# A linear-attention layer on eight cores: four of five weight loads split into staged pieces on other queues

## The reference

```python
# x: (8, 4096, 1024) f32; all weights (1024, 1024) f32
def attn(x):                                  # causal linear attention, 16 heads of 64
    q, k, v = x @ Wq.T, x @ Wk.T, x @ Wv.T
    q, k = phi(rope(q)), phi(rope(k))         # phi(x) = elu(x) + 1
    # per token t: K_sum += k_t; KV += k_t (x) v_t; y_t = (q_t KV) / max(q_t . K_sum, 1e-6)
    return Y @ Wo.T
x = x + attn(layernorm(x))
x = x + layernorm(x) @ sign(Wf).T
```

## Time and profile before

| | us |
|---|---|
| median of the runs | 1230.93 |
| the profiled execution | 1231.27 |
| its span on the slowest core (core 2) | 1229.7 |
| spans of the 8 cores | 1224.3 to 1229.7 |
| busy in the span: TensorE / VectorE / ScalarE / GpSimd | 905.9 / 689.6 / 492.1 / 160.4 |

### The profile page before, as it was taken

The page is one execution under the profiler, slowest core; times in us unless marked ns, Lnnn a source line. Parts: engine busy times, 40 slices in busy tenths (PEclk is TensorE's granted clock), DMA queues, the critical chain, the costliest instruction groups (busy, mean ns, idle before and its releaser), DMA issues.

```text
span 1229.7 us, 33733 instructions; the slowest of 8 cores (1224.3 to 1229.7 us)
## 1 busy us (share of the span) xinstructions
PE 905.9 (74%) x13571; PEld 829.4 (67%) x13571; DVE 689.6 (56%) x1514; ACT 492.1 (40%) x991; POOL 160.4 (13%) x139
## 2 busy tenths in 40 slices
PE   1428787877878787787878778787777787877775
PEld 1417776766777676677767667777667776866775
DVE  5225555566555556655555665554566555556653
ACT  2134433444443344444334444433444434344341
POOL 1201110011111001111100111110011111001110
PEclk9859989899998989999898999988989989898996
DMA  9871011011000101010110111010011001001000
GB/s 167 129 117 36 19 37 36 19 36 36 33 22 36 36 18 36 36 36 19 36 36 19 36 36 36 19 36 28 26 36 37 28 27 36 25 30 36 19 13 24
DMA packets 15144, 46.77 MB, mean 38 GB/s; under 512 B 1424, under 2 KB 1424, under 8 KB 14992
## 3 DMA queue, kind: packets, MB, share of 16 engines
q1 hardware_dynamic: 9504, 33.62, 7.7%
q0 software_dynamic: 5488, 11.01, 5.9%
HBM read 38.86 MB, written 16.78 MB: 45 GB/s over the span
## 4 chain that ended last, share of the span: by engine, by line
DVE 29%; PE 27%; issue 23%; ACT 11%; DMA 6%; POOL 1%; DVEq 1%; ACTq 0%; POOLq 0%
PE att L496 6%; PE pjA L496 6%; PE pjB L496 6%; PE pjC L496 6%; DVE junkV L404 4%; DVE Asb L629 4%; DVE x L712 4%; DVE outb L728 3%; DMA wk<-wkT 3%; ACT kev L510 3%; ACT qT L475 2%; PE ptr L448 2%; DMA wf<-wfT 2%; DVE ln L441 2%; ACT YT L700 2%
## 5 line engine op out<-in xcount | busy, mean ns | idle before, releaser
L526 POOL TENSOR_TENSOR rA<-qev,tabS_s 128x512 bf16<-128x512 bf16 x32 | 37.0, 1157 | 882.9 <-ACT qev L510 813.0
L496 PE MATMUL att<-wo,YT 128*128 128x128 bf16 x544 | 98.8, 258 | 7.7 <-ACT YT L700 7.7
L496 PE MATMUL pjC<-wo,YT 128*128 128x128 bf16 x480 | 86.3, 255 | 23.2 <-ACT YT L700 23.2
L496 PE MATMUL pjA<-wo,YT 128*128 128x128 bf16 x544 | 98.3, 257 | 6.6 <-ACT YT L700 6.6
L496 PE MATMUL pjB<-wo,YT 128*128 128x128 bf16 x480 | 86.2, 254 | 5.7 <-ACT YT L700 5.7
L496 PE MATMUL att<-wv,ln1T 128*128 128x128 bf16 x512 | 68.1, 224 | 19.9 <-ACT kev L510 13.1
L496 PE MATMUL att<-wq,ln1T 128*128 128x128 bf16 x512 | 77.1, 228 | 6.2 <-DMA wq<-wqT 6.2
L496 PE MATMUL pjC<-wv,ln1T 128*128 128x128 bf16 x512 | 67.6, 220 | 17.9 <-ACT kev L510 17.9
L496 PE MATMUL pjB<-wf,ln2T 128*128 128x128 bf16 x512 | 77.8, 224 | 0.8 <-ACT ln2T L454 0.8
L496 PE MATMUL pjB<-wv,ln1T 128*128 128x128 bf16 x512 | 66.7, 219 | 15.4 <-ACT kev L510 15.4
L496 PE MATMUL pjA<-wv,ln1T 128*128 128x128 bf16 x512 | 66.5, 221 | 15.1 <-ACT kev L510 15.1
(11 more groups left out here) (152 smaller groups left out, 3043.6 us busy)
## 6 DMA issues: line engine op xcount, KB each, us to landing
xs<-x SPq DMA_DIRECT2D x32, 512.0 KB, 3.7
out<-outb SPq DMA_DIRECT2D x32, 512.0 KB, 2.6
wq<-wqT POOLq DMA_DIRECT2D x1, 2048.0 KB, 22.3
wk<-wkT POOLq DMA_DIRECT2D x1, 2048.0 KB, 34.1
wv<-wvT POOLq DMA_DIRECT2D x1, 2048.0 KB, 47.1
wo<-woT POOLq DMA_DIRECT2D x1, 2048.0 KB, 18.4
wf<-wfT POOLq DMA_DIRECT2D x1, 2048.0 KB, 25.8
tabS_s<-tabS POOLq DMA_DIRECT2D x1, 256.0 KB, 27.4
```

Source lines behind the costliest of these rows:

```text
L496: s.add("tensor", lambda e, o=o, i=i, pj=pj, off=off, lsb=lsb, w_sb=w_sb: e.matmul(pj[:, off:off + 128], lsb[:, i * 128:(i + 1) * 128], w_ ...
L526: s.add("gpsimd", lambda e: e.tensor_tensor(out=rAv, in0=HI, in1=Sb, op=ALU.mult), reads=[src_res, "tabS"], writes=["rA"], tag=f"{tag}_rA")
```

## The change

The load of wq stays one casting DMA on GpSimd. wk, wv, wo and wf are each cut in 8 pieces, one for each block of 128 input rows. A piece is a plain f32 DMA of 0.52 MB into a staging buffer, followed by a cast into the bf16 weight. wk and wv go through SyncE's queue into the two f32 buffers `x2` and are cast by VectorE; wo and wf go through ScalarE's queue into the two f32 buffers `outb` and are cast by ScalarE itself. Piece p therefore waits until piece p-2 on the same queue is cast. Each block of a weight becomes a resource of its own, and a matmul waits for its block `i` only. The sign over wf stays one instruction and reads all 8 blocks. The declared costs are 1400 for a piece's DMA, 800 for a cast on VectorE and 1400 on ScalarE.

```diff
-        for wsb, wdram, name, weng in ((wq, wq_d, "wq", "gpsimd"),
-                                       (wk, wk_d, "wk", "gpsimd"),
-                                       (wv, wv_d, "wv", "gpsimd"),
-                                       (wo, wo_d, "wo", "gpsimd"),
-                                       (wf, wf_d, "wf", "gpsimd")):
-            s.add(weng,
-                  lambda e, a=wsb, b=wdram: e.dma_start(
-                      out=a[:].rearrange("p (a o) -> p a o", a=8),
-                      in_=b.rearrange("(a p) o -> p a o", p=128)),
-                  writes=[name], dma=True, tag=f"load_{name}", cost=7000)
+        s.add("gpsimd",
+              lambda e: e.dma_start(
+                  out=wq[:].rearrange("p (a o) -> p a o", a=8),
+                  in_=wq_d.rearrange("(a p) o -> p a o", p=128)),
+              writes=[f"wqb{i}" for i in range(8)], dma=True,
+              tag="load_wq", cost=7000)
+        for wsb, wdram, name, qeng, ceng, stg in (
+                (wk, wk_d, "wk", "sync", "vector", x2),
+                (wv, wv_d, "wv", "sync", "vector", x2),
+                (wo, wo_d, "wo", "scalar", "scalar", outb),
+                (wf, wf_d, "wf", "scalar", "scalar", outb)):
+            for i in range(8):
+                sb = stg[i % 2]
+                sres = f"stg_{id(stg) % 97}_{i % 2}"
+                s.add(qeng,
+                      lambda e, sb=sb, b=wdram, i=i: e.dma_start(
+                          out=sb[:],
+                          in_=b.rearrange("(a p) o -> p a o", p=128)[:, i, :]),
+                      writes=[sres], dma=True, tag=f"load_{name}p{i}", cost=1400)
+                if ceng == "vector":
+                    fn = (lambda e, sb=sb, a=wsb, i=i:
+                          e.tensor_copy(a[:, i * D:(i + 1) * D], sb[:]))
+                else:
+                    fn = (lambda e, sb=sb, a=wsb, i=i:
+                          e.copy(a[:, i * D:(i + 1) * D], sb[:]))
+                s.add(ceng, fn, reads=[sres], writes=[f"{name}b{i}"],
+                      tag=f"cast_{name}p{i}", cost=800 if ceng == "vector" else 1400)
         s.add("scalar", lambda e: e.sign(wf[:], wf[:]),
-              reads=["wf"], writes=["wf"], tag="sign_wf")
+              reads=[f"wfb{i}" for i in range(8)],
+              writes=[f"wfb{i}" for i in range(8)], tag="sign_wf")
 ...
+            wresi = [f"{wres}b{i}" for i in range(8)]
 ...
-                        reads=[lresA if i < 4 else lresB, wres],
+                        reads=[lresA if i < 4 else lresB, wresi[i]],
```

## The result

The changed kernel takes 1241.15 us in the median of 11 runs, against 1231.3 before (10 runs). The ratio is 1.0075, 95% interval 1.006 to 1.0091: some 9 us slower, 7 to 11 by the interval. The forecast was 1228, a gain. The profiled execution took 1240.08 us, with a span of 1238.4 on core 0, against 1231.27 and 1229.7.

The account below looks back on a forecast made before the run. The prediction took a loading stage of about 92 us and 31 unchanged periods as the bound. From 1231.27 it took 6.2 us for an earlier YT and added 3.0 for exposed sign and casts: 1228.1, range 1214 to 1246.

Parts of the forecast that it names:

- What bounds the kernel: Whole kernel: a loading stage of about 92 us, then 31 chunk periods of 35.88 us on average, unchanged.
- Who gets the bandwidth: Loading stage: queues share 336 GB/s; wq lands at 24 to 30 us, wv's last piece at 71.
- The work of the DMA engines: Loading stage: 23.6 MB at 336 GB/s takes 70 us; last piece lands at 73 against 84.5 before.
- The path from wv to YT: Chunk 0: cast, v projection, evacuations and 7.7 us more put YT at 85.5 against 91.67, 6.2 us earlier.
- The sign and the casts: ScalarE behind YT: two casts and the sign, 9.2 us, meet a 6.33 us gap; 3 us exposed.
- ScalarE's list becomes the bound: Rival, loading stage: wo and wf pieces waited for singly, sign ahead of v's evacuation, YT at 103; 1235 to 1247, chance 0.13.
- Nothing is gained: Rival, loading stage: three lists leave as much loose DMA time; wv lands at 77, time 1230 to 1234, chance 0.17.
- The order of the periods: Rival, chunk periods: the schedule may settle in another order, 0.8 us per period, 25 us in all; chance 0.05.

Follow-up runs that it names:

- one-queue kernel: Kernel before, sign behind LN1 of chunk 1 and in eight pieces, all GpSimd loads issued ahead of rotations, seven DMA semaphores for three: 1214.92 us.
- held-back wo: Changed kernel with the first two pieces of wo issued only behind the last cast of wk: 1244.55 us.
- third buffer: Changed kernel with three staging buffers in place of two for wk and wv, x's loads for chunks 1 and 2 moving too: 1233.65 us.
- place of x: Changed kernel with two buffers, the loads of x for chunks 1 and 2 issued behind the pieces of wv: 1237.02 us.
- real costs: Changed kernel with planner costs near measured lengths, 3300 for a SyncE piece (was 1400), 30000 for wq (was 7000): 1242.94 us.

## Why the prediction was wrong

**What bounds the kernel.** Right: a loading stage and periods that don't change. The residual of chunk 1 carries the whole difference. In the profiled executions the forecast of 1228.1 missed 1240.1 by 12.0 us: 8.8 in YT of chunk 0, 4.6 in the sign and the casts behind it, less 1.4 in the rest.

**Who gets the bandwidth.** The step that failed. That queues share the engines was right, the sizes were not. The sum let wq land at 24 to 30 us and then gave SyncE's queue half of 336 GB/s: 14 pieces from 29 us at 3.1 us each. It began as forecast: by 28 us SyncE's queue had moved 2.58 MB of its 9.96. But all three queues together moved 305 GB/s there and not 336 (casting writes counted twice, as f32 read): 99 by SyncE's and 80 by ScalarE's, where 79 were taken for each, so 125 were left for the casting queue. wq landed at 37.2 (1.6 + 35.6) and the second table at 45.6, and from 29 us until then three queues shared where the sum had two. From 28 to 79.7 us SyncE's queue moved 144 GB/s in place of 168, so its pieces took 3.7 us each. wk's last cast was expected near 46 and came at 50.3, wv's at 70 to 73 and came at 79.7. With ScalarE's queue held back until wk was cast, the three moments were 28.3, 43.0 and 70.0, as forecast or earlier, and in the changed kernel the last cast of wv waits for its transfer and not for VectorE ([2.24 <-DMA x<-wvT]): the sharing made wv late. How much of the 8.8 us is the lower rate and how much the third queue is not separated. The Trainium skill (DMA: Bandwidth & Descriptors, "Issuing engines are not separate DMA queues") says that queues of different issuers interleave on the same engines and save only issue time. These runs agree with the interleaving. They show besides that a queue at whose head an urgent load stands loses time to the others: wq took 22.3, 26.7 and 35.6 us beside ever more traffic.

**The work of the DMA engines.** "At 336 GB/s that is 70 us" was too short twice over. At the 305 GB/s of 2 to 28 us, at a share of 1.00, even full engines need 77 us and end at 80. And from 45 us on they were not full, so the last piece of wf was cast at 98.4 and not at 73. The lower bound of the sum was used as its value. This did not make wv late, since wv came at 70.0 in a kernel whose engines were emptier still (0.59 from 45 to 80 us), but it put the last casts of wf and the sign behind YT. The one-queue kernel shows that 77 us can be reached: only with everything issued ahead and nothing waiting for a cast.

**The path from wv to YT.** From 79.7 the prediction's own terms give 79.7 + 0.7 + 4.5 + 1.3 + 7.7 = 93.9, and YT came at 94.31. This chain was sized well; the 8.8 us between "6.2 earlier" and "2.6 later" all lie in wv's landing. But counting an earlier YT one for one as time was not sound: with only the sign moved YT came 16.8 us earlier and the kernel gained 9. The lower end of the range, 1214, rests on that step.

**The sign and the casts.** The second term that was too small: 3 us exposed, and 7.6 measured (4.9 + 2.7). The sign alone costs 6.0 (without it 1235.1), and two casts of wf hold the transposed LN1 for another 2.3 (5.0 us behind YT in place of 2.7). The mechanism was named, and the gap of 6.33 us was taken as room for casts and sign. But that gap is TensorE's projection time, which starts only when the transposed LN1 is there, so a cast ahead of it moves the gap and hides nothing; and chunk 0's state copies and chunk 2's statistics already filled 3.7 us of it.

**The rivals.** Of the numbers the one called "ScalarE's list becomes the bound", 1235 to 1247, held 1241. Its mechanism was half right: ScalarE's pieces went at 6.1 us each (16 by 98.4), above the 4.5 from which it was to decide, but the sign stood behind v's evacuation, not ahead of it, and YT came at 94, not at 103; that its number fits is in part luck. "Nothing is gained" had the moment of wv nearly right (77, the last piece was there at 79.7) and the time wrong, because it had no term for the sign and the casts. The order of the periods did not change. ScalarE's list should have had more weight, since the prediction had found that one misplaced entry of it had held YT for 16 us before. The range ended at 1246 and held the time; the direction was wrong.

**What stays open.** How the 23% of loose DMA time from 45 to 80 us divides between two pieces in flight, waits on casts and the order of the lists: the held-back wo, the third buffer, the place of x and the real costs each moved wv, but each moved the lists as well. And how the sign costs 2.3 us one period later: the lower granted clock stands beside it, and no run changes the clock alone.

## What to carry to other kernels

When one queue already fills the DMA engines, more queues don't load faster; they change who waits. So put loads on one queue in the order of need, issue them all at the start, and look whether semaphores or other work on the issuing engine hold the later ones back. Before judging a change, ask what the kernel before wastes that the change removes by accident: here moving one 7 us instruction in a list gave 9 us, and the split loads had to pay back that gain before they showed as a loss. A cast in pieces on an engine with an in-order list puts as many waits into that list as there are pieces, and every one of them can hold something urgent. A gap in an engine's list is room only for what nothing else is waiting to fill.

## What the runs showed of the hardware

A queue's share depends on what the other queues carry. Beside one plain queue that loaded wk, with no ScalarE queue, wq took 26.7 us, beside two 35.6, and beside two with three pieces in flight on one of them 41.6. From 2 to 28 us the casting queue had 62%, 44% and 39% of the DMA engines' time. Per full share the casting queue read 282 GB/s of f32 from 2 to 28 us of the changed kernel, and 307 alone from 60 to 84.5 us before; SyncE's and ScalarE's plain transfers moved 307 and 343 from 2 to 28 us and 292 and 315 from 45 to 80. So the cast on the way took little of the DMA engines' time (8 to 18% in the one window that has both) and no instruction of another engine, while the change spends 32 casts on VectorE and ScalarE.
